# Dense attention over 16 heads: all query-key products on VectorE, six of sixteen weighted values summed on TensorE, GpSimd only weighs

## The reference

```python
def _L0_attn_b_ref(x, Wq, Wk, Wv, Wo, bo):
    N, S, D = x.shape                      # 8, 256, 128; H = 16 heads of hd = 8
    q = (x @ Wq.T).reshape(N, S, H, hd).transpose(0, 2, 1, 3)
    ...
    att = jnp.einsum('nqhd,nkhd->nhqk', q, k)
    att = jax.nn.softmax(att / jnp.sqrt(jnp.asarray(hd, x.dtype)), axis=3)
    out = jnp.einsum('nhqk,nkhd->nqhd', att, v).reshape(N, S, D)
    return out @ Wo.T + bo
```

## Time and profile before

| what | value |
|---|---|
| median of 3 runs | 4089.36 us (4086.76 to 4089.8) |
| profiled execution | 4093.68 us |
| its span, first to last instruction | 4091.9 us |
| mean granted TensorE clock over the span | 0.965 |
| first projection of the dense attention | at 2041.18 us of the span |
| last division of its rounds | at 2152.58 us, 0.49 us long |

### The profile page before, as it was taken

One profiled execution on the slowest core, in us unless ns is written; L12 is line 12 of the kernel. 1 busy time (PEld: TensorE's weight loads), 2 busy tenths in 40 slices (PEclk: granted clock), 3 DMA queues, 4 the chain that ended last, 5 costly groups with the idle time before them and its releaser, 6 DMA issues. The chain is left out here.

```text
span 4091.9 us, 139809 instructions
## 1 busy us (share of the span) xinstructions
PE 3767.2 (92%) x51875; PEld 2247.0 (55%) x51875; DVE 3550.8 (87%) x11427; ACT 3327.1 (81%) x10473; POOL 3075.6 (75%) x4007
## 2 busy tenths in 40 slices
PE   6888889999999999999867999999999999996676
PEld 2333346666666666666553666666666666663464
DVE  7999989999999999999487999999999999975646
ACT  6888689999999999999515999999999999993122
POOL 3999788888888888888396888888888888762314
PEclk8999999999999999999898999999999999997887
DMA  1000111111112111111002111111111111110000
GB/s 30 1 1 1 48 25 34 44 34 39 44 28 54 31 36 49 26 36 34 12 1 64 26 36 46 29 50 35 31 48 35 44 31 39 31 26 3 6 3 11
DMA packets 78603, 122.65 MB, mean 30 GB/s; under 512 B 26024, under 2 KB 47204, under 8 KB 77924
## 3 DMA queue, kind: packets, MB, share of 16 engines
q1 hardware_dynamic: 77924, 113.71, 10.7%
HBM read 35.56 MB, written 1.05 MB: 9 GB/s over the span
## 5 line engine op out<-in xcount | busy, mean ns | idle before, releaser
L1131 POOL TENSOR_TENSOR local_qk<-local_qk,local_rb 128x512 f32<-128x512 f32 x768 | 973.2, 1278 | 88.5 <-DVE local_rb L1541 88.5
L1427 ACT ACTIVATE local_pr<-local_tb,local_nmax 128x96 f32<-128x96 f32 x3072 | 1010.5, 379 | 24.6 <-DVE local_nmax L1560 14.1
L1237 PE MATMUL local_pj<-local_wqkv,local_xs 128*64 128x512 f32 x3072 | 814.1, 609 | 21.5 <-DVE local_rb L1541 8.3
L1164 POOL TENSOR_TENSOR local_pr<-local_pr,local_rsum 128x384 f32<-128x384 f32 x768 | 623.0, 828 | 274.4 <-DVE local_rsum L1567 274.4
L1560 DVE CUSTOM_DVE_ANT_0 local_tb<-local_tb,local_mask,local_rinv 128x96 f32<-128x96 f32 x3072 | 772.6, 319 | 14.5 <-PE local_tb L1262 14.0
L1427 ACT ACTIVATION_READ_ACCUMULATOR local_pr<-local_tb,local_nmax 128x1 f32 x3072 | 753.1, 245 | 0.0
L1538 DVE TENSOR_TENSOR local_qk<-local_pj,local_rope 128x512 f32<-128x512 f32 x768 | 517.4, 674 | 113.7 <-ACT local_sq L1410 108.5
L1548 DVE TENSOR_REDUCE local_ss<-local_sq 128x8 f32<-128x512 f32 x768 | 521.8, 680 | 32.0 <-ACT local_sq L1410 32.0
L1410 ACT ACTIVATE local_sq<-local_pj 128x512 f32<-128x512 f32 x768 | 491.6, 640 | 55.6 <-PE local_pj L1237 55.3
L1541 DVE TENSOR_TENSOR local_rb<-local_pj,local_rope 128x512 f32<-128x512 f32 x768 | 523.0, 681 | 3.4 <-POOL local_qk L1131 3.4
L1286 PEld LDWEIGHTS local_ob<-local_prT,local_v 128*64 128x64 f32 x12288 | 413.9, 138 | 137.8 <-issue 55.4
(11 more groups left out here) (461 smaller groups left out, 7252.6 us busy)
## 6 DMA issues: line engine op xcount, KB each, us to landing
local_v<-local_v SPq DMA_DIRECT2D x288, 256.0 KB, 3.8
local_wqkv<-L_ffn_Wqkv_dram SPq DMA_DIRECT2D x72, 256.0 KB, 2.8
local_wo<-L_ffn_Wo_dram SPq DMA_DIRECT2D x12, 512.0 KB, 4.0
local_w<-L_ffn_W_dram SPq DMA_DIRECT2D x12, 341.0 KB, 2.9
mamba_parts<-mamba_in_low SPq DMA_DIRECT2D x24, 64.0 KB, 2.0
local_w<-L_ffn_W_dram SPq DMA_DIRECT2D x12, 128.0 KB
y_dram<-store_xtok SPq DMA_DIRECT2D x4, 256.0 KB, 2.8
local_oT<-rope_dram SPq DMA_DIRECT2D x2, 256.0 KB, 2.8
```

Source lines behind the costliest of these rows:

```text
L1131: nc.gpsimd.tensor_tensor(qk[:, u, :], qk[:, u, :], rb[:, u % 2, :], ALU.add).then_inc(s["summed"], 1)
L1164: nc.gpsimd.tensor_tensor(at, at, view(rsum[:, k // 2, k % 2, 0:1], [[1, 4], [0, KW]]), ALU.mult).then_inc(s["weighted"], 1)
L1237: ins = nc.tensor.matmul(bank[own, :], xs[:, par, u // 4 * P + own.start:u // 4 * P + own.stop], wqkv[:, dep % 2, u % 4 * BANK:(u % 4 + 1) ...
L1427: ins = nc.scalar.activation(pr[:, (NU * c + k) % PR_RING, i, WIN:WIN + KW], scores[:, i * KW:(i + 1) * KW], ACT.Exp, scale=-1.0, bias=nma ...
```

## The change

GpSimd's `part` goes; VectorE's `multiply(t)` makes all 2048 products. `sum_values(t)` is divided: TensorE adds six of the sixteen weighted values of each output with six matmuls of 128 columns against the identity, each reading every sixteenth word of `pv`; VectorE reduces the other ten to `rest` (1280 products to 128 sums, in SBUF), and a seventh matmul adds `rest` to the same PSUM accumulation, which `divide` then reads. The output sums get two PSUM banks in place of two halves of one. TensorE's order is one round further ahead in the scores, with the value sums of round t behind the scores of round t + 1; VectorE's order begins a round with `maxima(t + 1)` and has `multiply(t + 2)` after `invert(t)`.

```diff
-    A_DVE = 13
+    KEYS_PE = 6
...
+        rest = m.sb("rest", [P, 2, P])
...
-        o = bank[6]
+        o = [bank[6], bank[7]]
...
             def sum_products(t):
-                pe.wait_ge(s["prod_dve"], t + 1)
-                pe.wait_ge(s["prod_pool"], t + 1)
+                pe.wait_ge(s["multiplied"], t + 1)
                 need(pe, s["shifted"], t - 1)
...
+            def sum_values(t):
+                values = pv[:, t % 2, :].rearrange("p (o b) -> p o b", b=NH)
+                pe.wait_ge(s["weighed"], t + 1)
+                need(pe, s["o_ready"], t - 1)
+                for b in range(KEYS_PE):
+                    nc.tensor.matmul(o[t % 2][:, 0:P], net.ident[:, :], values[:, :, b], start=(b == 0), stop=False)
+                pe.wait_ge(s["rest_ready"], t + 1)
+                nc.tensor.matmul(o[t % 2][:, 0:P], net.ident[:, :], rest[:, t % 2, :], start=False, stop=True).then_inc(s["u_ready"], 1)
+
             for t in range(3):
                 project(t)
+            sum_products(0)
             for t in range(SLO):
                 if t + 3 < SLO:
                     project(t + 3)
-                sum_products(t)
+                if t + 1 < SLO:
+                    sum_products(t + 1)
+                sum_values(t)
...
-            part(0)
-            part(1)
             for t in range(SLO):
-                if t + 2 < SLO:
-                    part(t + 2)
                 weigh(t)
...
             def multiply(t):
                 dve.wait_ge(s["qkv_ready"], t + 1)
                 need(dve, s["summed"], t - 1)
-                products(nc.vector, t, 0, A_DVE, bank[t % 4][:, 0:1]).then_inc(s["prod_dve"], 1)
+                q = view(qkv[:, t, 0:1], [[1, HD], [HD, NH], [0, NH]])
+                k = view(bank[t % 4][:, 0:1], [[1, HD], [0, NH], [HD, NH]], C)
+                nc.vector.tensor_tensor(pq[:, t % 2, :, :, :], q, k, ALU.mult).then_inc(s["multiplied"], 1)
...
             def sum_values(t):
                 dve.wait_ge(s["weighed"], t + 1)
-                need(dve, s["o_ready"], t - 1)
-                nc.vector.tensor_reduce(o[:, t % 2 * P:(t % 2 + 1) * P], pv[:, t % 2, :].rearrange("p (o b) -> p o b", b=NH), AX.X, ALU.add).then_inc(s["u_ready"], 1)
+                need(dve, s["u_ready"], t - 1)
+                nc.vector.tensor_reduce(rest[:, t % 2, :], pv[:, t % 2, :].rearrange("p (o b) -> p o b", b=NH)[:, :, KEYS_PE:NH], AX.X,
+                                        ALU.add).then_inc(s["rest_ready"], 1)
...
             maxima(0)
             for t in range(SLO):
+                if t + 1 < SLO:
+                    maxima(t + 1)
                 sum_probs(t)
+                invert(t)
                 if t + 2 < SLO:
                     multiply(t + 2)
-                invert(t)
-                if t + 1 < SLO:
-                    maxima(t + 1)
                 sum_values(t)
                 if t:
                     divide(t - 1)
```

More of the change, by code:

```diff
@@ L1725, in dense_attention @@
         e = [bank[4], bank[5]]
-        o = bank[6]
-        names = ("projected qkv_ready prod_dve prod_pool summed maxed shifted exped psummed inverted "
-                 "weighed u_ready o_ready turned yT_ready out_ready").split()
+        o = [bank[6], bank[7]]
+        names = ("projected qkv_ready multiplied summed maxed shifted exped psummed inverted "
+                 "weighed rest_ready u_ready o_ready turned yT_ready out_ready").split()
         s = {n: net.sem(f"{tag}_{n}") for n in names}
@@ L1735, in project @@
                 need(pe, s["qkv_ready"], t - 3)
-                need(pe, s["prod_dve"], t - 3)
+                need(pe, s["multiplied"], t - 3)
                 tokens = view(net.zT[:, 0, 0:1], [[SLO, P]], t)
@@ L1772, in copy @@
                 act.wait_ge(s["projected"], t + 1)
-                need(act, s["prod_dve"], t - 3)
+                need(act, s["multiplied"], t - 3)
                 nc.scalar.activation(qkv[:, t, :], bank[t % 4][:, 0:3 * C], ACT.Copy).then_inc(s["qkv_ready"], 1)
@@ L1791, in _ @@
                 nc.scalar.activation(yT[:, :, 4 * q:4 * q + 4, :], view(bank[q][:, 0:1], [[SHI, B], [P, 4], [1, SHI]]), ACT.Copy).then_inc(s["yT_ready"], 1)
[L1793 to L1798, removed]
         @block.gpsimd
         def _(pool):
[L1802 to L1805, removed]
             def weigh(t):
@@ L1856, in divide @@
                 dve.wait_ge(s["u_ready"], t + 1)
-                nc.vector.tensor_tensor(o_all[:, :, t, :], o[:, t % 2 * P:(t % 2 + 1) * P].rearrange("p (a c) -> p a c", c=HD),
+                nc.vector.tensor_tensor(o_all[:, :, t, :], o[t % 2][:, 0:P].rearrange("p (a c) -> p a c", c=HD),
                                         view(inv[:, t % 2, 0:1], [[1, NH], [0, HD]]), ALU.mult).then_inc(s["o_ready"], 1)
```

## The result

The changed kernel takes 4152.43 us (median of 5 runs, 4149.4 to 4154.8) against 4089.8 us before, measured beside it (5 runs, 4086.76 to 4093.94): 62.6 us more, a ratio of 1.0152 with a 95% interval of 1.0138 to 1.0166. The profiled execution took 4152.43 us.

What follows compares the result with a forecast made beforehand. GpSimd bounded the rounds before (6.43 us); afterwards a ring through TensorE and VectorE would (9.72 us). Ring +44.3, stepped reading +4.2, clock +17 make +65.5 on 4089.4: 4155 us, range 4130 to 4178.

Steps and rivals of the forecast that it cites:

- GpSimd bounds the rounds before, and freeing it gives room: Sixteen rounds: GpSimd has no gap in 6.43 us; without its 1.06 us product share it needs 5.38 us.
- The in-order list of TensorE closes a ring: The next scores queue behind the seventh matmul, which waits for `rest`; VectorE waits for those scores: +44.3 us in all.
- Ring V: Seventh matmul, projection, scores, maxima, multiply, `rest`: TensorE's 4.67 plus VectorE's 5.05 us, 9.72 us a round.
- the path through ScalarE: From `rest` through seventh matmul, projection, copy, exponentials and weighing to the next `rest`: 9.0 us, shorter by 0.7 and hidden.
- ring S: Named after measuring: weighing, six value sums, seventh matmul, projection, copy, exponentials, next weighing; 10.39 us in the changed kernel's timeline.
- the signs that were named: Expected in the new profile: 10 to 12 us rounds, seventh matmul waiting for `rest`, 5.4 us scores in most rounds, others.
- Value sums at a step of 16 words cost double: TensorE's six value sums take 2.6 us instead of 1.3, holding the seventh matmul back 0.35 us a round: +4.2 us.
- The clock: ten falls on the scores: TensorE's clock falls to 1.2 GHz in ten of 13 rounds, 1.69 us each on the scores: +17 us.
- Rival 1: The ring with a clock that holds: +44 to +48, 4134 to 4138 us; chance 0.25.
- Rival 2: The ring with a clock that stays low: +97 or so, 4186 us; chance 0.07.
- Rival 3: No ring, faster: TensorE's 5.6 us with packed reading sets the round, -9, 4080 us; chance 0.04.
- Rival 4: No change: the gain on GpSimd and a partial ring cancel; chance 0.02.

Runs made afterwards that it cites:

- experiment 8: Kernel before the change, with VectorE making all 2048 products and GpSimd only weighing; orders and value sums as they were: 4083.5 us, ratio 0.9982.
- experiment 3: Changed kernel with TensorE's value sums one round later: 4107.95 us, ratio 1.0042.
- experiment 10: Changed kernel with TensorE's value sums one round later and VectorE's order as before the change: 4095.63 us, ratio 1.0020.
- experiment 6: The kernel of experiment 1 with 20 unread bf16 matmuls between the six value sums and the seventh matmul: 4145.25 us, ratio 1.0138.
- experiment 5: Changed kernel with 22 unread bf16 matmuls behind each round's scores, to hold the clock up: 4146.4 us, ratio 1.0139.
- experiment 2: Changed kernel with VectorE's order as before the change (multiply ahead of maxima): 4152.08 us, ratio 1.0151.
- experiment 4: Changed kernel with pv laid out key head first, so value sums read adjacent words and VectorE's reduction steps by 128 words: 4178.05 us, ratio 1.0216.
- experiment 12: Changed kernel with value sums one round later, VectorE's order as before, and value sums reading adjacent words of pv: 4079.54 us, ratio 0.9981.
- experiments 9: Changed kernel with TensorE's value sums one round later and reading adjacent words of pv: 4101.59 us, ratio 1.0030.
- experiment 1: Changed kernel with ScalarE listing exps(t) ahead of copy(t + 3): 4169.26 us, ratio 1.0190.

## Why the prediction was right, and where its sum was off

The forecast was 4155 us in 4130 to 4178, measured 4152.43. By its steps:

- **GpSimd bounds the rounds before, and freeing it gives room.** Right: experiment 8 moves the share to VectorE and changes nothing else, and gains 0.2% (interval 0.1 to 0.3%).
- **The in-order list of TensorE closes a ring.** Right: experiment 3 moves three lines and takes back 44 of 62.6 us, and experiment 10 is at work-bound rounds.
- **Ring V, 9.72 us, is the longer; the path through ScalarE, 9.0 us, is hidden.** Wrong in the second half. Ring V is 9.81 us at full clock (experiment 6), but ring S is 10.24 (experiment 5) and binds: experiment 2 shortens V and nothing moves. The failed step is the 9.0 us: it ended with weighing and `rest` 1.49, though the seventh matmul also stands behind the six value sums. The prediction charged the six with 0.35 us over ring V (10.07 in all) and didn't see that with 2.78 us in place of 1.49 the other path becomes a ring of its own which VectorE isn't part of. By the prediction's own terms (its 7.53, less the 0.05 behind `rest`, plus 2.6 for the six) that ring is 10.08 us: the round came out near the measured 10.24 though it was booked as a delay of the wrong ring. Two of the signs that were named did not appear: the seventh matmul waits for `rest` in only 3 of 16 rounds, and scores of 5.4 us in most rounds were seen once (5.31 us). The others came about as told, as VectorE's 5.16 us at the maxima and GpSimd's 4.97 us of idle time.
- **Value sums at a step of 16 words cost double.** Right: 2.78 us for the twelve instructions with the clock at full (experiment 10, granted clock 1.00), 1.50 with adjacent words (experiment 4, also 1.00). The row of L2460 was the right one to go by.
- **The clock: ten falls on the scores, +17 us.** The term that was mis-sized. Falls there were, in 14 of the 16 rounds on the value sums, and from there in part on the seventh matmul and the projection; all falls together cost 6.6 us. The 16 score instructions took more than 4 us in only two of the rounds, as TensorE's timeline of the changed kernel has it:

```profile
2135.58 4.48 PE L1746 MATMUL dense_attn_bank<-dense_attn_pq,net_ident 128*128 128x256 f32 x16
...
2197.62 5.31 PE L1746 MATMUL dense_attn_bank<-dense_attn_pq,net_ident 128*128 128x256 f32 x16
```

So the total came near by luck, through two errors of opposite sign: ring too short by 4.0 us, clock too dear by 10.4. For the 15 steps the prediction had 137.9 + 4.2 + 17 = 159.1 us; measured were 146.1 of ring (142.1 predicted) and 6.6 of clock, 152.7. With 1.9 us later at the first `rest`, 1.1 more behind the last and 1.0 less ahead of the first projection, plus 2.2 less in the rest of the program, the spans differ by 152.7 - 94.2 + 1.9 + 1.1 - 1.0 - 2.2 = 58.3 us. Behind the last `rest` the prediction had 0.4 us less where 1.1 more was measured, for the same reason: the six value sums stand ahead of the seventh matmul. Of the other 4.3 us between this and the medians' 62.6, 3.9 are the spread from one execution to another (the profiled one before took 4093.68, the median is 4089.8), and 0.4 lies outside the spans.
- **Rival 1, a clock that holds** was given +44 to +48 and lost: experiment 5, where it holds, is still 57 us above before. Without the clock the ring alone, being S, costs that much, and 4146.4 is still 8 us above the 4138 that this rival allowed. **Rival 2, a clock that stays low,** is refuted by the granted clock of 1.00 behind the value sums. **Rival 3, no ring,** is refuted by the wait rows; as a kernel it exists in experiment 12, at 4079.54 where the rival had 4080, though by VectorE's 5.91 us a round and not TensorE's 5.6. **Rival 4,** no change, is excluded by the interval, 1.0138 to 1.0166.

The Trainium skill (TensorE: Matmul & The Clock Gate, the part on what each phase is for) says that matmuls stay in program order, and here the trace agrees: `sum_products(t + 1)`, its products made 3.1 us before (2108.96 + 2.23 against 2114.28), never starts ahead of the seventh matmul.

## What to carry to other kernels

When work moves to an engine with an in-order list, don't only add up its busy time: walk from each waiting instruction to what is queued behind it and on to who waits for that, until you are back at the start; in this kernel the longest such ring was the round, 10.4 us where the busiest engine, TensorE, had some 7.0 us of work (experiment 10). Walk all rings, with every instruction ahead of the waiting one (the six here), since cutting one only uncovers the next, and a part that costs 17 us alone can be half of what gives 44. And when an order leaves TensorE waiting, see in which instructions the low clock then falls: moving the gap by a few microseconds cost more than it saved.

## What was not expected of the hardware

- A 128-column float32 matmul instruction whose moving operand steps by 16 words takes about as long at either clock level: twelve in 2.78 us at the full level (experiment 10, from 2095.48, granted clock 1.00), 2.96 at the low one (changed kernel, from 2110.44, granted clock 0.50); from the first one's start to the seventh matmul's that is 2.60 and 2.78 us. That is why falls on the value sums were cheap, while the scores, with adjacent words, went from 3.62 to 5.3 and more.
- VectorE's reduction of 1280 elements took 1.47 us with ten adjacent words at a time and 2.28 us with a step of 128 words (experiment 4). In experiments 9 and 12 it took 2.37 us at the same step; why was not looked into.
- GpSimd's 2048 products went from 5.42 to 4.06 us when the values were read at adjacent words instead of at a step of 8, with each exponential repeated instead of read at adjacent words (experiment 4); the products are written to adjacent words in both kernels. The Trainium skill (GPSIMD Engine Reference, performance pitfalls for Q7 kernels) says that reads at a step of over 8 bytes cost about half as much again; the trace has 1.34 times, for both reads changed at once.
- Work that nobody needs can pay: 20 extra matmuls a round made experiment 1 faster by 24 us.
